# A transformer block in six passes: open joints between passes, one shared identity, products by quarters in the recurrence, and the last rounding in halves

## What is computed

```python
x = x + tanh(g_xattn[0]) * L0_xattn(layernorm(x), fside, fside, ctx_1024)
x = x + tanh(g_ffn[0])   * L0_ffn(layernorm(x))     # quantised linear, 3-tap conv, silu, quantised linear
x = x + tanh(g_xattn[1]) * L1_xattn(layernorm(x), ctx_1024, ctx_1024)
x = x + tanh(g_ffn[1])   * L1_ffn(layernorm(x))
```

```python
def step(c, xt):
    ft = sigmoid(xt @ wf.T + c @ uf.T + bf)
    it = sigmoid(xt @ wi.T + c @ ui.T + bi)
    gt = tanh(xt @ wc.T + c @ uc.T + bc)
    return ft * c + it * gt, None
c_final, _ = lax.scan(step, c0, x)
h = tanh(einsum('tbi,oi->tbo', x, wo) + c_final @ uo.T + bo)
```

## Time and profile before

| | us |
|---|---|
| median of 3 runs | 2549.83 |
| lowest, highest | 2549.44, 2553.63 |
| the profiled execution | 2550.44 |
| its span in the trace | 2548.7 |
| its mean granted TensorE clock | 0.968 of 2.4 GHz |
| attention, from its first to its last instruction, about | 88 to 977 |
| feed-forward | 978 to 1487 |
| context attention | 1488 to 1888 |
| recurrence | 1889 to 2451 |
| output | 2452 to 2548.7 |

### The profile page before, as it was taken

One profiled execution on the slowest core, in us unless ns is written; L12 is line 12 of the kernel. 1 busy time (PEld: TensorE's weight loads), 2 busy tenths in 40 slices (PEclk: granted clock), 3 DMA queues, 4 the chain that ended last, 5 costly groups with the idle time before them and its releaser, 6 DMA issues. The chain is left out here.

```text
span 2548.7 us, 40730 instructions
## 1 busy us (share of the span) xinstructions
PE 2326.8 (91%) x16307; PEld 1545.2 (61%) x16348; DVE 1390.9 (55%) x1717; ACT 1060.3 (42%) x1228; POOL 607.2 (24%) x213
## 2 busy tenths in 40 slices
PE   8899999999999987899999779999878999999989
PEld 6655554555555544455555346766656888888867
DVE  7665646556555444777777567677534222222235
ACT  5445445454454442555555544444433222211223
POOL 0045546455464651000000013323210000000000
PEclk9899999999999988999999989999988999999989
DMA  9410101101010103111111221222231000000046
GB/s 299 183 40 12 50 10 48 43 11 47 10 49 11 42 30 113 45 51 50 55 56 34 69 79 58 73 81 77 93 115 55 33 33 33 33 18 32 17 165 215
DMA packets 102014, 163.73 MB, mean 64 GB/s; under 512 B 16996, under 2 KB 39524, under 8 KB 99102
## 3 DMA queue, kind: packets, MB, share of 16 engines
q1 hardware_dynamic: 95918, 150.82, 17.9%
q10 hardware_dynamic: 6000, 11.54, 1.2%
HBM read 112.63 MB, written 49.71 MB: 64 GB/s over the span
## 5 line engine op out<-in xcount | busy, mean ns | idle before, releaser
L1152 DVE TENSOR_REDUCE att_mx<-att_sn 128x2 f32<-128x1024 f32 x196 | 239.8, 1223 | 150.8 <-PE att_sn L961 148.9
L1061 ACT ACTIVATE att_num<-att_st 128x2048 f32<-128x2048 f32 x128 | 240.5, 1879 | 148.2 <-PE att_st L942 89.6
L865 POOL TENSOR_TENSOR att_es<-att_es,att_num 128x2048 f32<-128x2048 f32 x64 | 294.6, 4604 | 15.0 <-ACT att_num L1061 8.7
L861 POOL TENSOR_TENSOR att_es<-att_num 128x2048 f32<-128x2048 f32 x32 | 145.8, 4557 | 366.0 <-PE att_pj L922 341.6
L2541 ACT ACTIVATE rec_ga<-rec_g,rec_bg 128x512 f32<-128x512 f32 x84 | 57.1, 687 | 309.2 <-PE rec_g L2442 309.2
L2442 PE MATMUL rec_g<-weights_a_h,row_weights_h 128*128 128x512 f32 x384 | 153.6, 400 | 14.0 <-ACT rec_ga L2541 11.1
L2442 PE MATMUL rec_g<-weights_a_l,row_weights_h 128*128 128x512 f32 x384 | 152.1, 396 | 0.0
L2442 PE MATMUL rec_g<-weights_a_h,row_weights_l 128*128 128x512 f32 x384 | 151.8, 395 | 0.0
L562 POOL TENSOR_TENSOR ffn_ln_rstd<-ffn_ln_var,ffn_ln_power 128x4 f32<-128x4 f32 x8 | 22.0, 2755 | 464.0 <-DVE ffn_ln_var L584 464.0
L1475 PE MATMUL ffn_h<-ffn_xqt,ffn_w 128*128 128x512 bf16 x486 | 116.3, 382 | 16.3 <-DVE ffn_hs L1736 12.8
L2063 POOL TENSOR_TENSOR xat_pr<-xat_e,xat_rd 128x1232 f32<-128x1232 f32 x32 | 72.9, 2278 | 244.2 <-DVE xat_rd L2266 237.5
(11 more groups left out here) (407 smaller groups left out, 5800.6 us busy)
## 6 DMA issues: line engine op xcount, KB each, us to landing
rows<-in_x SPq DMA_DIRECT2D x16, 1024.0 KB, 5.4
rows<-x SPq DMA_DIRECT2D x16, 1024.0 KB, 5.2
rows_b<-in_fside_BxSxS SPq DMA_DIRECT2D x8, 1024.0 KB, 7.9
heads<-att_o SPq DMA_DIRECT2D x32, 256.0 KB, 2.3
weights_b_l<-heads SPq DMA_DIRECT2D x8, 1024.0 KB, 5.3
x<-ffn_xr SPq DMA_DIRECT2D x32, 256.0 KB, 2.1
xat_xr<-x SPq DMA_DIRECT2D x8, 1024.0 KB, 5.2
out_x<-x SPq DMA_DIRECT2D x8, 1024.0 KB, 8.8
```

Source lines behind the costliest of these rows:

```text
L861: pool.tensor_tensor(ES[:], E[0][:], E[1][:], ALU.add).then_inc(s_sum, 1)
L865: pool.tensor_tensor(ES[:], ES[:], E[k][:], ALU.add).then_inc(s_sum, 1)
L1061: act.activation(E[k][:], st_ps[:], ACT.Exp, scale=SCALE).then_inc(s_exp, 1)
L1152: dve.tensor_reduce(MX[c % 2][:, m // 2, 2 * DH * (m % 2):2 * DH * (m % 2) + DH + 1:DH], sn_ps[:], AX, ALU.max, negate=True).then_inc(s_ma ...
```

## The change

Seven things change.

1. The waits of SP for a pass's last stores at its end are gone (in attention, feed-forward, context attention). The semaphores that count these stores (`heads_stored`, `x2_stored`, `x3_stored`) live on into the next pass, whose engines wait for them where they first use or overwrite what is meant.
2. The identity is built once, in the first pass. Its bf16 copy is made by POOL early in attention (`lead.identb`). The three passes start without it and without PE's wait for it; the recurrence keeps a memset of `rec_ones`.
3. At the end of attention DVE scales the rows and finds their maxima ahead of the last quad's jobs. In the last quad POOL adds two tensors less one: 2 adds in place of 3, and PE adds the fourth exponential into the sums itself, with 4 matmuls more.
4. In each turn of the feed-forward `scaled(b, 6)` stands ahead of `ln.scale`.
5. In the last batch of the feed-forward the first of the four roundings, its widening by ACT and PE's wait for it go in two halves.
6. In the recurrence's first step the gates of m=0 are made quarter by quarter of the input channels, each as soon as its low half is there. The transposes of batch 1 stand between the gates of m=3 (quarters 0 and 1 ahead of gate 1, 2 and 3 ahead of gate 2), and ACT makes their high halves after the last gate's matmuls.
7. At the end of the recurrence the halves of `uo` and of the state's first three quarters are made while PE makes the last gates; the products go quarter by quarter into four banks. The halves of the state go into buffers of WX that are read no more.

```diff
@@ attention_pass, DVE
             def late():
                 ln.aggregate(dve, rows0)
-                for task in LATE:
-                    job(task)
                 dve.wait_ge(ln.s_rstd, B + 1)
...
                 lead.row_maxima(dve, F, rows0)
+                for task in LATE:
+                    job(task)
@@ attention_pass, PE
-                        last = pe.matmul(out[heads(j), :], ones[:], ES[:, j, :], start=True, stop=True)
+                        last = pe.matmul(out[heads(j), :], ones[:], ES[:, j, :], start=True, stop=not final)
+                        if final:
+                            last = pe.matmul(out[heads(j), :], ones[:], E[T - 1][:, j, :], start=False, stop=True)
@@ attention_pass, SP (so in quantised_ffn_pass and context_attention_pass)
-            sp.wait_ge(s_store, QUADS * 16)
@@ quantised_ffn_pass, POOL and PE
-            make_identity(pool, ident[:], s_ident)
-            pool.wait_ge(s_ident, 2)
-            pool.tensor_copy(identb[:], ident[:]).then_inc(s_ident, 1)
...
-            pe.wait_ge(s_ident, 7)
@@ quantised_ffn_pass, SP
             turn(1, True, True, True)
+            sp.wait_ge(heads_stored, B * C * 16)
@@ quantised_ffn_pass, DVE
                     rounded(b - 1, 3)
+                scaled(b, 6)
                 if front:
                     ln.scale(dve, b + 1, rows)
-                scaled(b, 6)
...
-            for group in range(GROUPS):
+            for half in range(2):
+                rounded_half(half)
+            for group in range(1, GROUPS):
                 rounded(B - 1, group)
+            def rounded_half(half):
+                own = slice(2 * half, 2 * half + 2)
+                dve.wait_ge(s_qb, B)
+                dve.wait_ge(s_quant, (B - 1) * GROUPS)
+                dve.tensor_tensor(S8[0][:, own, :], SS[:, own, :], QB[:].unsqueeze(1).broadcast_to([P, 2, S]),
+                                  ALU.mult).then_inc(s_half if half == 0 else s_scaled, 1)
@@ recurrence_pass, PE
             def first_turn():
-                pe.wait_ge(s_lo, C)
-                for m in range(C):
+                for k in range(C):
+                    pe.wait_ge(s_lo, k + 1)
+                    for n in range(3):
+                        for i, (a, c) in enumerate(((0, 0), (0, 1), (1, 0))):
+                            last = pe.matmul(g_ps[0][n][:], WX[n][a][:, k, 0:P], XT[c][:, k, :],
+                                             start=(k == 0 and i == 0), stop=(k == C - 1 and i == 2))
...
+                        if m == C - 1:
+                            for c in ((), (0, 1), (2, 3))[n]:
+                                transposed_rows(1, c)
...
-                for c in range(C):
-                    transposed_rows(1, c)
...
-            pe.wait_ge(s_clo, B * C)
             pe.wait_ge(s_wlo, NW)
-            for t in range(T):
-                if t >= 2:
-                    pe.wait_ge(s_ycd, t - 1)
-                split3(nc, pj_ps[t % 2][:], lambda h, k: CH[h][:, k, t * P:t * P + P],
-                       lambda h, k: WX[0][h][:, k, :], range(C)).then_inc(s_yc, 1)
+            pe.wait_ge(s_gt, 1 + (B - 1) * 12 + 9)
+            for k in range(C):
+                pe.wait_ge(s_clo, (B - 1) * C + k + 1)
+                for t in range(T):
+                    own = slice(t * P, t * P + P)
+                    for i, (a, c) in enumerate(((0, 0), (0, 1), (1, 0))):
+                        last = pe.matmul(y_ps[t][:], LAST_C[a][:, k, own], WX[0][c][:, k, :],
+                                         start=(k == 0 and i == 0), stop=(k == C - 1 and i == 2))
@@ recurrence_pass, ACT
+                    elif m == C - 1:
+                        act.wait_ge(s_wx, 1)
+                        high_half(act, NG + 1)
+                        act.wait_ge(s_wx, 2)
+                        for c in range(C - 1):
+                            state_high(act, b + 1, c, LAST_C)
```

More of the change, by code:

```diff
@@ L2221, in ahead @@
                 gates()
+                act.wait_ge(rows_stored, B * T * 16)
             def late():
@@ L2517, in rows_high, with high @@
                     act.wait_ge(s_lo, a * C)
+                def high(c):
+                    act.wait_ge(s_xw, a * C + c + 1)
+                    act.activation(XT[0][:, c, :], XW[:, c, :], ACT.Copy).then_inc(s_hi, 1)
+                second = isinstance(a, int) and a == 1
                 for c in range(C):
@@ L2603, in turn @@
                         rows_low(b + 1)
+                    if not more and m == 3:
+                        low_half(dve, NG + 1)
+                        for c in range(C - 1):
+                            state_low(dve, b + 1, c, LAST_C)
                     dve.wait_ge(s_gt, 1 + b * 12 + 3 * m + 1)
```

132 lines of the change are left out of this document (83 added, 49 removed).

## The result

The changed kernel took 2520.4 us (median of 4 runs, 2515.03 to 2523.41), the kernel before 2550.05 (4 runs, 2549.44 to 2553.63): 29.7 us less, ratio 0.9881 with a 95% interval of 0.9862 to 0.9899. The forecast was 2523.0 in 2516 to 2530. The profiled execution was the fastest of the four, 2515.03, with a span of 2513.2. So its trace shows 35.5 us less than that of before, 5.8 more than the medians do, and that difference has to be accounted for too.

The account below looks back on a forecast made before the run. PE, busy 91% of the span, was taken to bound the kernel. Terms summing to -26.8 us took the profiled 2550.44 to 2523.6; the median, 0.6 lower, gave 2523.0, range 2516 to 2530.

Parts of the forecast that it names:

- Attention to feed-forward: Gap of PE between these passes: -4.4 us by DVE's new order and fewer adds, -1.2 by starting without the identity.
- Pair 6: Feed-forward's six steady turns: scaling this pair ahead of the rows spares PE 0.97 us idle each, -5.8 us.
- Turn 0: Feed-forward's first turn, without a rounding: the new order makes pair 7 late and the convolution waits, +1.8 us.
- Halves: Feed-forward's last batch, first rounding in two parts: PE still waits for the last group, one more DVE instruction, +0.1 us.
- The two joints: Starts of context attention and of the recurrence: without SP's store wait and the identity, PE starts 2.3 us earlier at each.
- First step: Context attention to recurrence: PE's start 2.3 us and the gates 3.7 earlier; 1.7 to 4.1 remain, -4.1 taken.
- End of the first turn: Recurrence: transposes lie between gates and ACT makes the high halves after the last gate, -0.9 us (0 to -1.5).
- The tail: Recurrence's end: the last state's 48 products follow the gates without a break, 10.9 us instead of 20.9, -10.0 us.
- The clock: Rival: PE keeps 2.4 GHz behind shorter gaps at three places, 7.8 us more gained, 2515; chance 0.12.
- The swap's room of 0.8: Rival: pair 7 has 0.8 us of room at most, PE waits as long at the convolution, no gain, 2529; chance 0.12.
- the tail gave all: Against a rival: recurrence's last products give half, first quarters not split in time or PE starts slow, 2528; chance 0.08.
- the joints opened: Against a rival: barriers wait for another engine or SP's loads set the recurrence, 4.2 us lost, 2527; chance 0.10.

Follow-up runs that it names:

- three_adds: The changed kernel with POOL's third add in the last quad back and without PE's four extra sums; 2526.5 us, ratio 0.9888.

## Why the prediction was right

- **Attention to feed-forward**, -4.4 - 1.2 = -5.6: measured 5.95. The split was less good than the sum: DVE's part was 5.09, the identity's 0.85. Taking the order out loses 4.35, and taking the fewer adds out loses 3.15, so the order needs the power of the variance early, as the prediction had it (about 962.5, 1.3 us ahead of av's end; it came 1.32 ahead).
- **Pair 6**, "6 x 0.97 = -5.8": the mechanism was right, the term too small. It measured 1.15 a turn, 6.9 in all. The step that failed is taking the idle column as the whole price of a stall. POOL's power wasn't held up further by the scaled pair, as the prediction took it.
- **Turn 0**, +1.8: measured 1.74.
- **Halves**, +0.1: nothing to be seen above 0.2.
- **The two joints**, -2.3 each: 2.16 each, 1.67 of it the wait, 0.48 the identity.
- **First step**, in "I take -4.1": with the joint it was 5.0 (2.16, and 2.8: 30.9 to 32.1 in nine traces with the edit, mean 31.4, and 34.2 in three_adds, which had the longest low clock of these ten there, against 34.2 and 34.3). The mechanism was right: PE waits for the third gate's low half, in nine of the ten traces, for 0.4 to 1.9 us. The size was off. In "PE then waits until 1913.7" the low half moves by 1.7 with SP. It moved by 3.2: 27.3 us behind context attention's last product (1896.44), against 30.5 before, since its load was issued 1.9 earlier and landed in 5.2 us instead of 6.6. A part of the 2.8 may be the clock: the stretch had 6.8 and 7.0 us of it low without the edit, and less than 4.6 in seven of the ten with it. Before, PE came to these products 2.5 us after their low half (1915.40), and its own list set the first tanh:

```profile
1917.92 0.40 PE L2457 MATMUL rec_pj<-rec_wu2h,rec_cc 128*2 128x512 f32 x1
```

- **End of the first turn**, -0.9: 0.6 to 0.8.
- **The tail**, -10.0: 10.0; the stretch took 79.12 to 79.14 in 13 traces.
- **The clock**, not in the sum: the output pass no longer begins slowly, 1.6 in every trace with the new tail. I had it as a rival that "gives more", with 7.8 at three places; it gave something at this one alone. The prediction's "even short gaps cost" doesn't hold for it: PE idles 1.90 ahead of the output pass now and 1.88 before, and only before is the clock low behind it. What differs is the 7.17 us of idle 15.6 us earlier; that this is the cause is argued, not shown.

The parts as measured sum to -5.95 - 6.9 + 1.74 - 2.16 - 5.0 - 0.7 - 10.0 - 1.6 = -30.6, against -29.7 by the medians and -30.7 in the last batch. That is 3.8 more than the sum of -26.8: 1.6 for the output pass, 1.1 for pair 6 and 0.9 for the first step, and 0.35 for the attention's joint, less small ones. The range held because the missing terms were small against its width, and not because errors cancelled, but for the 0.7 and 0.35 within the attention's joint. The other 5 us by which the profiled execution was ahead of before's are the low clock in attention (3.5) and what else its stretches differ by.

Of the rivals only the clock's came, in part. The swap's room of 0.8 held, the tail gave all, the joints opened, and the low stretches didn't grow: mean granted clock 0.975 and 0.973 in the two traces, 0.968 before.

## What to carry to other kernels

Price a stall of PE by its idle time and the overlap that it breaks, the difference between a matmul's printed duration and its pitch. Where an engine waits for two things, shortening one pays only with the other: the reordered jobs on DVE and the shorter list on POOL were worth 5.09 together, and 1.95 and 0.75 alone. Where the clock's low stretches move with each execution, compare distances between the same two instructions of two traces, and use stretches without a low clock.

## What the runs showed of the hardware

The clock was low (1.2 GHz) for 164 us of the execution of before, at a mean of 0.968, and for 127 and 137 us of the changed kernel's two, at 0.975 and 0.973. The places differ between executions of one kernel: the stretch up to the last av took 952.4 and 956.7 us for the same code. Filling a gap of 6 us with 16 matmuls raised the granted clock behind it from 0.61 to 1.00 and lowered it from 0.91 to 0.64 some 50 us on. Behind a tail that real work filled, none of the 13 output passes started slowly; the one behind the old tail did.
